# Batched role adapter with layer norm on one core: first loads spread over two queues, no role check on SyncE, warm-up matmuls on a constant, row loads issued among later loads

## The reference

```python
# x: (8, 512, 1024); role: (8,); W_down: (3, 1024, 512); W_up: (3, 512, 1024)
h = einsum('bsh,bhk->bsk', x, W_down[role]) + b_down[role]
h = gelu(h, approximate=False)
u = einsum('bsk,bkh->bsh', h, W_up[role]) + b_up[role]
y = x + u
mean, var = mean(y, -1), mean(square(y - mean), -1)
out = (y - mean) * rsqrt(var + 1e-5) * gamma[role] + beta[role]
```

## Time and profile before

| what | value |
|---|---|
| median of 3 runs | 363.72 us |
| the 3 runs | 363.72, 366.36, 363.20 us |
| the profiled execution | 363.14 us |
| its span, first to last instruction | 361.3 us |
| mean granted TensorE clock | 0.995 |
| TensorE matmul busy | 353.2 us (98% of the span) |
| VectorE busy | 286.5 us (79%) |
| ScalarE busy | 183.4 us (51%) |
| moved by DMA | 96.59 MB, mean 267 GB/s |

### The profile page before, as it was taken

One profiled execution on the slowest core, in us unless ns is written; L12 is line 12 of the kernel. 1 busy time (PEld: TensorE's weight loads), 2 busy tenths in 40 slices (PEclk: granted clock), 3 DMA queues, 4 the chain that ended last, 5 costly groups with the idle time before them and its releaser, 6 DMA issues.

```text
span 361.3 us, 4949 instructions
## 1 busy us (share of the span) xinstructions
PE 353.2 (98%) x1547; PEld 289.7 (80%) x1547; DVE 286.5 (79%) x301; ACT 183.4 (51%) x298; POOL 59.2 (16%) x73
## 2 busy tenths in 40 slices
PE   8999999999999999999999999999999999999992
PEld 4888888888888888888888888888888888888881
DVE  4788889498993989759996699957989489893886
ACT  5784544861368414683256814476234862255131
POOL 0000132003220212102140022300232003320012
PEclk9999999999999999999999999999999999999997
DMA  7999989982999649894598927999199982745023
GB/s 229 400 409 410 366 317 354 343 315 80 314 334 366 240 115 365 281 387 187 176 378 296 380 106 221 373 309 355 77 293 358 336 320 81 239 147 203 1 116 116
DMA packets 27659, 96.59 MB, mean 267 GB/s; under 512 B 3202, under 2 KB 3714, under 8 KB 27650
## 3 DMA queue, kind: packets, MB, share of 16 engines
q1 hardware_dynamic: 23328, 81.54, 63.1%
q10 hardware_dynamic: 4322, 14.95, 10.6%
HBM read 79.70 MB, written 16.78 MB: 267 GB/s over the span
## 4 chain that ended last, share of the span: by engine, by line
PE 98%; DVE 1%; DVEq 0%; issue 0%
PE down_ps L287 48%; PE up_ps L294 48%; PE up_ps L393 1%; DVE h_full L650 0%; DVE rows L656 0%; DVE up_ps L633 0%; DVEq L43 0%; DVE squares L745 0%; DVE last_mean L643 0%; DVE neg_shift L641 0%; DVEq L632 0%
## 5 line engine op out<-in xcount | busy, mean ns | idle before, releaser
L287 PE MATMUL down_ps<-x_hi,wd_hi 128*128 128x512 f32 x256 | 82.0, 389 | 0.0
L287 PE MATMUL down_ps<-x_lo,wd_hi 128*128 128x512 f32 x256 | 81.9, 389 | 0.0
L287 PE MATMUL down_ps<-x_hi,wd_lo 128*128 128x512 f32 x256 | 81.9, 389 | 0.0
L294 PE MATMUL up_ps<-wu_lo,h_hi 128*128 128x512 f32 x256 | 79.5, 389 | 0.0
L294 PE MATMUL up_ps<-wu_hi,h_hi 128*128 128x512 f32 x256 | 79.4, 389 | 0.0
L294 PE MATMUL up_ps<-wu_hi,h_lo 128*128 128x512 f32 x256 | 79.4, 389 | 0.0
L542 POOL TENSOR_TENSOR var_eps<-var,eps 128x1 f32<-128x1 f32 x31 | 22.1, 714 | 292.2 <-ACT squares L448 292.2
L445 ACT ACTIVATE neg_mean_scaled<-row_sum 128x1 f32<-128x1 f32 x31 | 6.3, 203 | 122.3 <-DVE rows L617 122.3
L605 DVE TENSOR_TENSOR h_lo<-h_full,h_hi 128x512 fp32r<-128x512 f32 x32 | 22.2, 693 | 45.9 <-ACT h_hi L440 45.8
L287 PEld LDWEIGHTS down_ps<-x_hi,wd_hi 128*128 128x128 f32 x256 | 48.0, 188 | 10.7 <-issue 0.8
L287 PEld LDWEIGHTS down_ps<-x_hi,wd_lo 128*128 128x128 f32 x256 | 48.0, 188 | 10.0
(11 more groups left out here) (46 smaller groups left out, 255.1 us busy)
## 6 DMA issues: line engine op xcount, KB each, us to landing
wu_stage<-W_up SPq DMA_DIRECT2D x32, 512.0 KB, 6.9
rows<-x SPq DMA_DIRECT2D x32, 512.0 KB, 7.3
x_stage<-xT SPq DMA_DIRECT2D x30, 512.0 KB, 6.7
wd_stage<-W_down SPq DMA_DIRECT2D x30, 512.0 KB, 6.7
out<-rows ACTq DMA_DIRECT2D x28, 512.0 KB, 4.8
b_up_row<-b_up SPq DMA_DIRECT2D x8, 512.0 KB, 5.0
gamma_row<-gamma SPq DMA_DIRECT2D x8, 512.0 KB, 9.4
beta_row<-beta SPq DMA_DIRECT2D x8, 512.0 KB, 10.0
```

Source lines behind the costliest of these rows:

```text
L287: return pe.matmul(down_ps[:, kc, :], wd_part[:, n, c * K + kc * P:c * K + (kc + 1) * P], x_part[:, n, c * S:(c + 1) * S], start=start, st ...
L294: mm = pe.matmul(up_ps[:, t % 2, half], h_part[:, kc, t * P:(t + 1) * P], wu_part[:, kc, half], start=(kc == 0 and h_part is h_hi and wu_p ...
```

## The change

It has five edits.

1. x's second chunk is no longer issued by SyncE but by ScalarE, after the roles and before x's third chunk.
2. The first role is read on SyncE without the check of its bounds. (The other reads of roles keep theirs.)
3. ScalarE casts x's second chunk after the two halves of W_down's first chunk, not before them.
4. The warm-up matmuls read constants of 1.0, one element per partition that is read again for every column, written ahead of the kernel by GpSimd. VectorE's memset, its semaphore and TensorE's wait on it are gone.
5. `load_rows(b + 1, 0)` and `load_rows(b + 1, 1)` are issued between `load_ahead(b + 2, ..., 1)` and `load_ahead(b + 2, ..., 2)`, not after `load_ahead(b + 2, ..., 3)`. For the first and the last batch the order is as before.

```diff
@@ SyncE
+            def load_first_rows(b):
+                load_rows(b, 0)
+                load_rows(b, 1)
+
             def steps(b):
+
                 first, last = is_first(b), is_last(b)
                 role = load_role(sp, b)
-                load_rows(b, 0)
-                load_rows(b, 1)
                 if not first:
                     load_rows(b, 2)
                     sp.wait_ge(normed, NT * b)
...
                 if isinstance(b, int) and b + 2 == B:
+                    load_first_rows(b + 1)
                     return
                 role_after = load_role(sp, b + 2)
-                for i in range(NLOAD):
-                    load_ahead(b + 2, role_after, i)
+                load_ahead(b + 2, role_after, 0)
+                load_ahead(b + 2, role_after, 1)
+                load_first_rows(b + 1)
+                load_ahead(b + 2, role_after, 2)
+                load_ahead(b + 2, role_after, 3)
...
             load_first_x(0, 0, first_x_landed[0])
-            load_first_x(0, 1, x_landed[0])
             sp.wait_ge(roles_landed, 16)
-            first_role = load_role(sp, 0)
+
+            first_role = nc.s_assert_within(sp.value_load(roles_sb[0:1, 0:1]), min_val=0, max_val=R - 1,
+                                            skip_runtime_bounds_check_because="the value is checked on ScalarE")
...
             load_role_row(b_up_row, b_up, first_role, b_up_landed)
+            load_first_rows(0)
             steps(0)
@@ TensorE
-            pe.wait_ge(zeros_ready, 1)
             for _ in range(WARM_UP):
-                pe.matmul(up_ps[:, 0, 0:BANK], squares[:, 0:P], squares[:, 0:BANK], start=True, stop=True)
+                pe.matmul(up_ps[:, 0, 0:BANK], nc.const_aps.tensor(1.0, [P, P], BF16),
+                          nc.const_aps.tensor(1.0, [P, BANK], BF16), start=True, stop=True)
@@ ScalarE
             act.dma_start(roles_sb[:, :], roles).then_inc(roles_landed, 16)
 
+            act.dma_start(x_stage[:, 0, S:CPL * S], x_src(0)[:, 0, S:CPL * S]).then_inc(x_landed[0], 16)
             act.dma_start(x_stage[:, 1, 0:S], x_src(0)[:, 1, 0:S]).then_inc(first_x_landed[1], 16)
             act.wait_ge(constants_ready, 2)
             act.activation(unused[:, :], eps[:, :], ACT.Gelu)
             round_first(x_hi, x_stage, 0, slice(0, S), first_x_landed[0], first_x_hi)
-            round_first(x_hi, x_stage, 0, slice(S, CPL * S), x_landed[0], x_hi_ready)
             round_first(wd_hi, wd_stage, 0, slice(0, EARLY), early_wd_landed, early_wd_hi)
             round_first(wd_hi, wd_stage, 0, slice(EARLY, K), first_wd_landed[0], first_wd_hi)
+            round_first(x_hi, x_stage, 0, slice(S, CPL * S), x_landed[0], x_hi_ready)
@@ VectorE
-            dve.memset(squares[:, 0:BANK], 0.0).then_inc(zeros_ready, 1)
```

More of the change, by code:

```diff
@@ L148, in bass_role_adapter_layernorm @@
         first_var_eps_ready = sem("first_var_eps_ready")
-        zeros_ready = sem("zeros_ready")
         constants_ready = sem("constants_ready")
```

## The result

The changed kernel took 365.40 us in the median of 22 runs, the kernel before 363.68 in 22; the ratio is 1.0033 with a 95% interval of 1.0021 to 1.0045. It is slower by a third of a per cent. Its times fall in two groups: 8 runs from 363.74 to 364.02, and 14 from 365.06 up. Of the kernel before, 3 of 22 lie above 365. The median of the lower group, 363.81, is only 0.1 above that of the kernel before; the median of the upper one is 365.5. So the loss of the whole is mostly the share of executions in the upper group.

A forecast was written before the change was run, and what follows sets the result against it. TensorE bounds 98% of the span, so only time before the first true matmul (6.02) could be gained. A 0.3 us gain gave 362.84 (363.14 - 0.3), or 363.4 off the median; forecast between, 363.1; range 362.2 to 364.4.

The forecast's parts named there:

- The landing: W_down's early half, issued at 2.64, lands 2.0 to 2.5 us later, at 4.6 to 5.1, against 5.4 before.
- the lower end of 4.6 to 5.1: Early end of W_down's predicted landing, favoured because its early half would share with x's chunks, not queue behind them.
- the clock comes up later: Rival at the start, chance 0.12: true matmuls start before the clock is up, each at 0.426 and not 0.227 us.
- The sum: Start of true matmuls: warm-up ends 5.53, data at 5.1 to 5.65, so start 5.55; gain taken as 0.3 us.
- the 1.95 that I had given: Loss in us, ending at 365.1, if the constant warm-up doesn't rouse TensorE's clock at all.
- My reading of the start: Kernel before: warm-up and data end together, data 0.15 us later; clock up at about 6.2; full-speed start in effect 6.10.
- the 0.08 that I charged to it: Cost in us, at the first true matmuls, of the clock coming up only at about 6.2.
- TensorE waits for nobody: From 6.02 to 354.44, 348.4 us, TensorE has no waits; changed loads, casts or queues can't shorten that stretch.
- the start where I put it: First true matmul at 5.55, 0.47 us earlier than 6.02.
- the cast order: ScalarE's cast of x's second chunk moved behind W_down's frees ScalarE; at least 1.2 us of slack before its use.
- The check's 0.25 us: SyncE without the first role's check issues W_down's early half 0.25 us earlier, at 2.64 and not 2.89.
- 0.94: Chance given to the whole change measuring the same, within 1% (3.6 us); faster 0.02, slower 0.04.

The follow-up runs named there:

- x's third chunk out of the way: Changed kernel with x's third chunk issued by SyncE just ahead of W_down's second part; first true matmul at 5.67; median 363.49 us, ratio 0.9998.
- the queue edit alone: Kernel before with only x's second chunk moved to ScalarE's queue, cast order and warm-up as before; median 363.90 us.
- 16 warm-ups: Changed kernel with 16 warm-up matmuls and its other edits kept; median 364.16 us, ratio 1.0005.
- 6 warm-ups: Kernel before with 6 warm-up matmuls and not 11, loads unchanged; median 365.19 us, ratio 1.0032.
- the constant alone: Kernel before with only the warm-up matmuls reading constants, without the wait for zeros; median 363.53 us, ratio 0.9997.
- the other order in batch 0: Kernel before; in batch 0, tile 0's variance precedes part 1's casts, its norm and tile 1's sum precede part 1's splits; 363.39 us, ratio 0.9997.

## Why the prediction was wrong

**The landing** is the step that failed: "So it lands between 2.64 + 2.0 and 2.64 + 2.5, 4.6 to 5.1". It landed at 7.07. I took the time from issue to landing as belonging to the transfer, and bounded it by transfers with a different load around them. What is in flight beside it decides it. With x's third chunk out of the way W_down's first packet started at 3.59 and the early half landed at 5.10, at my bound; that this chunk beside it costs it time is shown. The kernel before had the second chunk of x in the same queue, ahead of the early half, and that looked like an obstacle; on the other queue it is a worse one, by the packets of all twelve profiles. How it is worse stays open. In the kernel before W_down got no bytes before 4 us either, and ScalarE's queue took as much of the engines' time from 4 to 5. Full engines aren't the whole reason: with the queue edit alone they are busy for 70% of that microsecond, and SyncE's queue still moves only 0.10 MB and not 0.22. The rule of the Trainium skill's DMA: Bandwidth & Descriptors, "Queues, rings and completion order", that the engines take turns between the queues, agrees with the rows from 4 to 5 us, where both queues move packets, in both kernels. Just so, turns alone don't tell why the changed one is slower there, and my reading, that they speak for the lower end of 4.6 to 5.1, was wrong.

The profile overstates this step. Its landing is 1.6 us late; but where no group above 365 is in play, the medians are only 0.1 us (the changed kernel's lower group) to 0.6 us (16 warm-ups) above the kernel before. The rest of the 1.7 comes with the upper group.

**The clock** is the step that was half seen. The rival "the clock comes up later" was put for a start at 5.55 that came too early for it, with 0.12. What happened is that the start came too late: a gap, behind which the clock fell (here from 8.65 to 12.0) or hadn't come up yet. The sum had no term for a gap between the warm-up's end and the data. The price was 1.6 us in the changed kernel and 1.7 with the queue edit alone, under the 1.95 that I had given, and 2.7 with 6 warm-ups, above it. The 16 warm-ups take the upper group away with the data late, and the 6 warm-ups make it with the data in time; that is shown. That the length of the gap decides is argued: in the profiles the gap is 2.2 us for the changed kernel and 0.4 for the constant alone, with 13 of 22 and 1 of 12 slow spans, but a gap of 1.9 once passed without a fall. I should have asked what the warm-up is for: it holds the clock until the data come, so moving its end forward needs data that come forward as well. On its own, though, the constant did nothing that could be measured.

My reading of the start was off here, too. I took the 0.31 us between the first two true matmuls for a clock that came up at 6.2. But from the first pair to the second it is 0.54 in every profile that starts at the high clock, also with 16 warm-ups, where the clock had been up since 3.5. The last warm-up took 0.594 us and not 0.634, so the clock came up just before 6.0 (an estimate), and the 0.08 that I charged to it was not there to be won.

**"TensorE waits for nobody [...], so [...] it can only make it longer"** was right for the changed kernel, but the other half wasn't looked at: by how little nobody waits. The last up tile of batch 0 had about 0.2 us of slack, so more than that was not to be had from an earlier start. With the start where I put it (5.55, 0.47 earlier) about 0.2 us would have gone there, an estimate from the slack. In the run that started at 5.67, whose loads came 0.6 later, 0.4 went.

**What was right.** The first warm-up at 0.76 (0.84 predicted), its end at 5.49 (5.53), 0.43 apart, so a constant's column costs the same; the early issue at 2.58 (2.64); the first cast at 3.58 (3.60); the cast order; the moved rows worth nothing, as they were alone. Part 2 of x was issued 7.7 us later in its batch, a little beyond the 2 to 7 predicted, and landed, at 6.9 us by the median, about 8 us ahead of its cast. The check's 0.25 us were 0.31 and were worth nothing. And the change is within 1%, where 0.94 stood; the median, 365.4, lies 1.0 above the range, which took in neither late data nor a gap.

## What to carry to other kernels

A transfer's time from issue to landing belongs to what is in flight beside it. When the engines have much to do, ask which bytes go first, over all queues, and hold back those that aren't needed yet: here an early issue and another queue gave nothing, and holding back 256 KB brought the landing forward by 1 to 2 us. A warm-up and the load that it covers are one thing: when the load moves, check the gap, and let the warm-up be a little too long. And a busy engine with no waits may still have next to no slack: before costing an earlier start, take the slack of each later hand-over, above all where it hangs on a saturated DMA.

## What was not expected of the hardware

After an idle stretch of 2.2 us TensorE's first four matmuls ran at 2.4 GHz, and only then the clock fell to 1.2 GHz for 3.4 us; after one of 1.9 us in the run with 16 warm-ups it didn't fall. With 6 warm-ups 3 of 12 runs still took 363.2 to 363.4. The Trainium skill says in TensorE: Matmul & The Clock Gate, "The HAM clock gate (the "warmup" mystery)", that the moment of the change varies from run to run; these runs agree: the clock came up at about 3.5 us (16 warm-ups), 4.4 (the other order in batch 0) and 6.3 (x's third chunk late), in executions with a warm-up from 0.76 or 1.18. The granted clock of the profile's rows reads 1.00 in these slow stretches all the same, with 6 warm-ups up to 11.8 us, and 0.50 only for the fall in the changed kernel, so the spacing of the matmuls is the surer reading.
